# Two 16-head cross attentions: layer normalisation per batch, its shift by a product of two tensors, no opening product in the mixing, the last batch scaled by VectorE

## The reference, cut to what matters

```python
def cross_attention(x, context, w_q, b_q, w_k, b_k, w_v, b_v, w_o, b_o):   # context: (32, 77, 96)
    q = (x @ w_q + b_q).reshape(B, 128, 16, 8)          # 16 heads of 8
    k = (context @ w_k + b_k).reshape(B, 77, 16, 8)
    v = (context @ w_v + b_v).reshape(B, 77, 16, 8)
    scores = jnp.einsum('bqhd,bkhd->bhqk', q, k) / sqrt(8)
    weights = jax.nn.softmax(scores, axis=-1)
    out = jnp.einsum('bhqk,bkhd->bqhd', weights, v).reshape(B, 128, 128)
    return out @ w_o + b_o

x = layernorm(x + cross_attention(x, context, ...))     # (x - mean) / sqrt(var + 1e-5), no scale or bias
```

## Time and profile before

| | us |
|---|---|
| median of 3 runs | 3539.06 (3532.92 to 3542.62) |
| profiled execution, its own time | 3534.11 |
| its span, first to last instruction | 3532.3 |
| first cross attention, 1359.9 to 1560.6 | 200.7 |
| second cross attention, 3178.0 to 3378.7 | 200.7 |

### The profile page before, as it was taken

How to read it: one execution, slowest core, us unless ns; L and a number is a source line. 1 busy time by engine, 2 the same in 40 slices (tenths; PEclk the granted TensorE clock), 3 DMA queues, 4 the chain that set the end, 5 groups by cost and what they waited for, 6 DMA issues and landing times. The chain is left out here.

```text
span 3532.3 us, 80927 instructions
## 1 busy us (share of the span) xinstructions
PE 2729.6 (77%) x30395; PEld 1966.6 (56%) x30395; DVE 2442.8 (69%) x7116; ACT 1969.3 (56%) x3739; POOL 1545.0 (44%) x1205
## 2 busy tenths in 40 slices
PE   2899999987875957889899999956655656858846
PEld 1677777656564945556455555534433446845546
DVE  6688888866564968966666776649982553568945
ACT  2577777744443854765455655555432733556747
POOL 3555455412237823520165556623231257815544
PEclk9999999999976978989999999977766858978958
DMA  4333333311202211000000000000007012200013
GB/s 137 56 55 54 56 54 56 50 60 66 83 16 62 78 52 67 2 2 1 1 2 3 3 3 2 3 1 19 19 28 220 13 41 64 82 27 38 2 32 101
DMA packets 103278, 151.13 MB, mean 43 GB/s; under 512 B 26266, under 2 KB 76524, under 8 KB 101756
## 3 DMA queue, kind: packets, MB, share of 16 engines
q1 hardware_dynamic: 91546, 123.11, 14.1%
q0 software_dynamic: 10912, 22.70, 1.9%
q10 hardware_dynamic: 434, 0.15, 0.0%
HBM read 81.13 MB, written 49.04 MB: 37 GB/s over the span
## 5 line engine op out<-in xcount | busy, mean ns | idle before, releaser
L473 DVE TENSOR_REDUCE MX<-banks 128x8 f32<-128x1152 f32 x128 | 173.0, 1352 | 103.7 <-PE banks L290 103.6
L2469 POOL TENSOR_TENSOR SM<-SM,RZ 128x1232 f32<-128x1232 f32 x64 | 143.9, 2248 | 166.4 <-DVE RZ L2511 166.4
L1729 POOL DMA_INDIRECT sorted_rows<-SRC,IDX x160 | 156.7, 979 | 132.4 <-DVE IDX L1858 85.8
L442 POOL TENSOR_TENSOR KT<-KT,FL 128x512 f32<-128x512 f32 x64 | 81.6, 1275 | 304.0 <-DVE FL L462 304.0
L1742 POOL DMA_INDIRECT expert_results<-Y,DST x181 | 177.1, 979 | 81.8 <-DVE DST L1925 36.3
L399 ACT COPY PT<-banks 128x384 f32<-128x384 f32 x384 | 170.1, 477 | 48.6 <-PE banks L300 44.9
L1511 PE MATMUL banks<-XC,WR 128*128 128x128 f32 x1448 | 197.0, 280 | 0.2 <-ACT XC L1631 0.2
L300 PE MATMUL banks<-sb_c_ident,SM 128*128 128x128 f32 x1152 | 182.7, 286 | 9.8 <-ACT PT L399 9.4
L1511 PEld LDWEIGHTS banks<-XC,WR 128*128 128x128 f32 x1448 | 180.4, 196 | 2.5 <-ACT XC L1631 2.1
L2808 POOL TENSOR_TENSOR KQ<-T,EX 128x1024 f32<-128x1024 f32 x32 | 76.0, 2376 | 207.4 <-ACT EX L2789 207.4
L486 DVE TENSOR_TENSOR SM<-banks,MX 128x512 f32<-128x512 f32 x256 | 163.4, 679 | 0.0
(11 more groups left out here) (568 smaller groups left out, 8634.9 us busy)
## 6 DMA issues: line engine op xcount, KB each, us to landing
FL<-RAW SPq DMA_DIRECT2D x512, 64.0 KB, 2.3
sorted_rows<-in_zeros_dram SPq DMA_DIRECT2D x33, 528.0 KB, 8.5
XR<-sorted_rows SPq DMA_DIRECT2D x181, 66.0 KB, 1.9
SRC<-expert_results SPq DMA_DIRECT2D x16, 512.0 KB, 7.2
T<-s4d_k_dram SPq DMA_DIRECT2D x8, 1024.0 KB, 9.4
weight_region<-in_l_ffn__wall_dram SPq DMA_DIRECT2D x1, 4112.0 KB
film_dram<-F SPq DMA_DIRECT2D x8, 512.0 KB, 2.9
FO<-film_dram SPq DMA_DIRECT2D x8, 512.0 KB, 4.6
```

What stands on the lines that cost most here:

```text
L473: nc.vector.tensor_reduce(MX[:, n % 2], sc, AXX, ALU.max).then_inc(s.mx, 1)
L1729: nc.gpsimd.indirect_dma_start(out=rows, out_offset=bass.IndirectOffsetOnAxis(ap=IDX[:, k, t:t + 1], axis=0), in_=SRC[:, t, k, :], in_offs ...
L2469: nc.gpsimd.tensor_tensor(SM[:, t % 4], SM[:, t % 4], bc(RZ[:, t % 2, :].unsqueeze(2), [P, H, L]), ALU.mult).then_inc(s.nm, 1)
```

## The change

The normalisation of a group of four becomes four normalisations of one batch. At every step VectorE does one `bn_stats` and one `bn_aggr`, ScalarE one logarithm, one exponential and one application. The shift changes its form: ScalarE makes -mean by an `activation` with scale -1, and VectorE multiplies two [128, 1] tensors in SBUF with `tensor_tensor`. The zero product in front of the mixing goes, and the first product of each 32 rows opens its own sum instead. The multiplication of the last batch's weights by RZ moves from GpSimd to VectorE. The loops of VectorE and ScalarE run two steps longer.

```diff
+def dve_ln_stats_one(nc, dve, E, s, t, src):
+    st, mv = E.ln_stats[t // GB][:, t % GB, :], E.ln_mv[t // GB][:, t % GB, :]
+    nc.vector.bn_stats(st, src).then_inc(s.ln_stats, 1)
+    dve.wait_ge(s.ln_stats, t + 1)
+    nc.vector.bn_aggr(mv, st).then_inc(s.ln_var, 1)
+def act_ln_rstd_one(nc, act, E, s, t):
...
+    act.wait_ge(s.ln_var, t + 1)
+    nc.scalar.activation(std, mv[:, 1:2], ACT.Ln, bias=E.eps5[:]).then_inc(s.ln_std, 1)
+    nc.scalar.activation(st[:, 0:1], mv[:, 0:1], ACT.Identity, scale=-1.0)
+    act.wait_ge(s.ln_std, t + 1)
+    nc.scalar.activation(rstd, std, ACT.Exp, scale=-0.5).then_inc(s.ln_rstd, 1)
+def dve_ln_shift_one(nc, dve, E, s, t):
...
+    dve.wait_ge(s.ln_rstd, t + 1)
+    nc.vector.tensor_tensor(std, st[:, 0:1], rstd, ALU.mult).then_inc(s.ln_core, 1)
+def act_ln_apply_one(nc, act, E, s, t, src, dst):
...
+    act.wait_ge(s.ln_core, t + 1)
+    return nc.scalar.activation(dst, src, ACT.Identity, bias=std, scale=rstd)
...
-                        nc.tensor.matmul(z_bank, ZERO[:], ZERO[:], start=True, stop=False)
...
-    ins = nc.tensor.matmul(z_bank[32 * c:32 * (c + 1)], value_window(g, b, 4 * c + q), PT[:, t % 2, q, c, :], start=False, stop=q == 3)
+    ins = nc.tensor.matmul(z_bank[32 * c:32 * (c + 1)], value_window(g, b, 4 * c + q), PT[:, t % 2, q, c, :], start=q == 0, stop=q == 3)
...
-                    if i >= 8 and (i - 8) % GB == 0:
-                        act_rstd(nc, act, E, s, (i - 8) // GB)
-                    if i >= 9 and (i - 9) % GB == 0:
-                        g = (i - 9) // GB
-                        act_ln_apply(nc, act, E, s, g, grp(XB, g), grp(E.x, g))
+                    if 6 <= i < NB + 6:
+                        act_ln_rstd_one(nc, act, E, s, i - 6)
+                    if i >= 8:
+                        act_ln_apply_one(nc, act, E, s, i - 8, XB[:, i - 8, :], E.x[:, i - 8, :])
...
-                nc.gpsimd.memset(ZERO[:], 0.0).then_inc(s.one, 1)
...
-                    normalise(t)
+                    if t < NB - 1:
+                        normalise(t)
...
+                    if i == NB:
+                        t = i - 1
+                        dve.wait_ge(s.rz, t + 1)
+                        nc.vector.tensor_tensor(SM[:, t % 4], SM[:, t % 4], bc(RZ[:, t % 2, :].unsqueeze(2), [P, H, L]), ALU.mult).then_inc(s.nm_last, 1)
...
-                    if i >= 7 and (i - 7) % GB == 0:
-                        g = (i - 7) // GB
-                        dve.wait_ge(s.res, GB * (g + 1))
-                        dve_ln_stats(nc, dve, E, s, g, grp(XB, g))
-                    if i >= 9 and (i - 9) % GB == 0:
-                        dve_ln_shift(nc, dve, E, s, (i - 9) // GB)
+                    if 5 <= i < NB + 5:
+                        dve.wait_ge(s.res, i - 4)
+                        dve_ln_stats_one(nc, dve, E, s, i - 5, XB[:, i - 5, :])
+                    if 7 <= i < NB + 7:
+                        dve_ln_shift_one(nc, dve, E, s, i - 7)
```

More of the change, by code:

```diff
@@ L140, in act_ln_apply @@
     return ins
+def dve_ln_stats_one(nc, dve, E, s, t, src):
[4 more added lines that the diff above has]
+def act_ln_rstd_one(nc, act, E, s, t):
+    st, mv = E.ln_stats[t // GB][:, t % GB, :], E.ln_mv[t // GB][:, t % GB, :]
+    std, rstd = E.ln_std[t // GB][:, t % GB:t % GB + 1], E.ln_rstd[t // GB][:, t % GB:t % GB + 1]
+    act.wait_ge(s.ln_var, t + 1)
[4 more added lines that the diff above has]
+def dve_ln_shift_one(nc, dve, E, s, t):
+    st, std, rstd = E.ln_stats[t // GB][:, t % GB, :], E.ln_std[t // GB][:, t % GB:t % GB + 1], E.ln_rstd[t // GB][:, t % GB:t % GB + 1]
+    dve.wait_ge(s.ln_rstd, t + 1)
+    nc.vector.tensor_tensor(std, st[:, 0:1], rstd, ALU.mult).then_inc(s.ln_core, 1)
+def act_ln_apply_one(nc, act, E, s, t, src, dst):
+    std, rstd = E.ln_std[t // GB][:, t % GB:t % GB + 1], E.ln_rstd[t // GB][:, t % GB:t % GB + 1]
+    act.wait_ge(s.ln_core, t + 1)
+    return nc.scalar.activation(dst, src, ACT.Identity, bias=std, scale=rstd)
 def dve_ln_affine(nc, dve, E, s, k, src, dst, scale, shift):
@@ L2291, in xattn16 @@
     TAIL = 4 * L
-    with sublayer(nc, "xt_ps xt k_ps k kd v_ps v one q_ps q s_ps mx sub ex sm rz nm pt_ps pt z_ps zt o_ps rb res w_ld" + LN) as (s, ctx):
+    with sublayer(nc, "xt_ps xt k_ps k kd v_ps v one q_ps q s_ps mx sub ex sm rz nm nm_last pt_ps pt z_ps zt o_ps rb res w_ld" + LN) as (s, ctx):
         sb = E.scratch(ctx)
@@ L2296, in xattn16 @@
         MX = sb("MX", [P, 2, H]); SM = sb("SM", [P, 4, H, L]); PT = sb("PT", [P, 2, 4, 4, P])
-        ZERO = ctx.enter_context(nc.sbuf_tensor(f"zero_{nc.next_id()}", [1, P], BF16))
         SU = sb("SU", [P, 2, H]); RZ = sb("RZ", [P, 2, H]); ZT = sb("ZT", [P, 2, P])
@@ L2349, in weights_T @@
                     if a == 0:
-                        pe.wait_ge(s.nm, t + 1)
+                        if t < NB - 1:
+                            pe.wait_ge(s.nm, t + 1)
+                        else:
+                            pe.wait_ge(s.nm_last, 1)
                     if 2 * t + a >= 1:
@@ L2437, in weights @@
                     nc.scalar.copy(PT[:, t % 2, 2 * a:2 * a + 2].rearrange("k q c (r p) -> k (q c) r p", r=2), turned).then_inc(s.pt, 1)
-                for i in range(NB + 6):
+                for i in range(NB + 8):
                     t = i - 3
@@ L2455, in _ @@
                         nc.scalar.activation(SM[:, i % 4], SM[:, i % 4], ACT.Exp, scale=float(D) ** -0.5).then_inc(s.ex, 1)
-                    if i >= 8 and (i - 8) % GB == 0:
-                        act_rstd(nc, act, E, s, (i - 8) // GB)
-                    if i >= 9 and (i - 9) % GB == 0:
-                        g = (i - 9) // GB
-                        act_ln_apply(nc, act, E, s, g, grp(XB, g), grp(E.x, g))
+                    if 6 <= i < NB + 6:
+                        act_ln_rstd_one(nc, act, E, s, i - 6)
+                    if i >= 8:
+                        act_ln_apply_one(nc, act, E, s, i - 8, XB[:, i - 8, :], E.x[:, i - 8, :])
             @block.gpsimd
             def _(pool):
-                nc.gpsimd.memset(VZ[:], 0.0)
-                nc.gpsimd.memset(ZERO[:], 0.0).then_inc(s.one, 1)
+                nc.gpsimd.memset(VZ[:], 0.0).then_inc(s.one, 1)
                 def normalise(t):
```

## The result

| | before | after |
|---|---|---|
| median of the runs, us | 3535.99 (3525.19 to 3542.62, 4 runs) | 3590.73 (3588.16 to 3595.88, 4 runs) |
| ratio to before | | 1.016, 95% interval 1.013 to 1.0189 |
| profiled execution, span, us | 3532.3 | 3594.0 |
| first, second cross attention, us | 200.7, 200.7 | 230.5, 231.3 |

The changed kernel is 1.6% slower. The kernel before has a fourth run here (3525.19), which brings its median from 3539.06 down to 3535.99; the medians lie 54.7 us apart. The profiled executions lie 61.7 us apart, and that of the changed kernel is the slowest of its four. Of these 61.7 us of span, 29.9 and 30.6 lie in the two cross attentions (1364.19 to 1594.71 and 3207.89 to 3439.16), 1.3 in all the rest of the program.

The account below looks back on a forecast made before the run. VectorE was taken to set the pace, busy 19.98 of 21.0 us. Held shifts +66.9, statistics +1.5, zero vector -0.4 and end -3.8 gave +64.2 us, forecast 3600; own range 3588 to 3640, 8 in 10 3578 to 3655.

Parts of the forecast that it names:

- The held shift: VectorE's shift waits about 1.9 us for GpSimd's multiplication at 25 steps per cross attention, 6.80 us each; +66.9 us together.
- The bounds that I had left: Limits for a one-column shift's duration beside GpSimd: 0.15 us if not held, 1.9 if held throughout; upper end taken.
- The dividing line: Claim that VectorE instructions with two SBUF inputs are held beside GpSimd; a tensor_tensor with one PSUM input is not.
- The small terms: Parts beside the hold: statistics +1.5 us, zero vector's clearing -0.4, end -3.8; zero product and last batch 0.
- the zero product: Dropping it from TensorE's mixing gains nothing in the pipeline; at most -13 us if TensorE set the pace.
- the last batch: Its multiplication on VectorE, 1.44 us for GpSimd's 2.25, is hidden: 0, at most -0.8 us each time.
- Statistics, end and zero vector: Statistics at steps 5 and 6 +1.5 us; shorter end of both sublayers -3.8; clearing the zero product's operand gone -0.4.
- the 25 gaps: Intervals between reciprocals of batches 6 and 31 in each cross attention; forecast 170.6 us, before 138.3 and 136.0.
- The sum: All terms together, 66.9 + 1.5 - 0.4 - 3.8 = +64.2 us on the profiled execution's 3534.1.
- The rival with TensorE as bound: TensorE sets the pace if its clock falls below 0.68; at 0.60, +45 us, 3645; chance 0.10.
- The hold over the group's work: Hold also lasts through GpSimd's bias and keys, 3.5 us at 6 steps per sublayer, +42 us; chance within 0.02.
- The rival in which the shift passes: The one-column shift is not held beside GpSimd, taking 0.15 us: -10 us, median some 3529; chance 0.13.

Follow-up runs that it names:

- e1: Changed kernel with the shift as a one-column tensor_scalar, rstd as scalar operand, at the same place; 3516.3 us, ratio 0.9959.
- e2: Changed kernel with the same tensor_tensor shift directly behind the reciprocal, ahead of the residual addition and statistics; 3519.5 us, ratio 0.9965.
- e3: Changed kernel with the shift made by ScalarE and no VectorE instruction for it; 3512.3 us, ratio 0.9946.
- e4: Changed kernel with the one-column shift as scalar_tensor_tensor, still two SBUF tensors, at the same place; 3592.8 us, ratio 1.0171.
- e7: e3 with the zero product and its vector's clearing on GpSimd put back; 3512.27 us, ratio 0.9953.
- e5: Kernel before, without the zero product and with the last batch's weights multiplied on VectorE, normalisation unchanged; 3526.1 us, ratio 0.9996.
- e8: Changed kernel with GpSimd's multiplication of a batch's weights split into two instructions of 8 heads; 3548.4 us, ratio 1.0056.
- e10: e6 with the group's shift moved right behind the subtraction of the same step, 1.77 us sooner; 3511.4 us, ratio 0.9955.
- e11: e6 with a group's four applications on ScalarE spread over four steps, one each; 3513.4 us, ratio 0.9957.
- e6: Kernel before with the group's shift as four one-column tensor_scalar instead of one scalar_tensor_tensor of four columns; 3536.4 us, ratio 1.0005.

## Why the prediction was right

The forecast was 3600, the median is 3590.7, near the lower end of the range of 3588 to 3640 and on the side forecast.

**The held shift**: right in place, length and count. 1.87 us against 1.9; a step of 6.80 against 6.80; 170.1 against 170.6; +65.9 against +66.9. e1, e2, e3 and e4 show that the hold alone makes the loss: e4, which keeps it, has 3592.8; without it or with a fifth of its holds, all else left per batch, the same chip gives 3512.3 to 3519.5, some 73 to 81 us less. The bounds that I had left, 0.15 us to 1.9, were both real, for a `tensor_scalar` and a `tensor_tensor`; to go by the row of the same place was right. The dividing line was too simple: two inputs in SBUF are held, but so is a `tensor_scalar` of four columns with one (L2845). The forecast does not hang on that, because the shift of the changed kernel has two.

**The small terms**: the zero product at nothing is right where VectorE sets the pace (e7); for the last batch, and for both in the kernel before, e5 leaves up to some 6 us open. Statistics, end and zero vector together I put at -2.7; the two sublayers outside the 25 gaps came out at 60.4 - 65.9 = -5.5. Up to the reciprocal of batch 6 it is +0.7; the other -6.2 lie behind that of batch 31, where I had -3.8. The last addition to the end is 3.23 us for 3.4 forecast, so the rest lies in how the last batches run through. Which edit gave it I did not separate.

**The sum**: +61.7 in the spans for +64.2. Most of the 9 us by which 3600 is too high is the base: I went up from the profiled execution of before by 2 us to a median, and that of the changed kernel lies 5 below its profiled 3595.88.

**The rival with TensorE as bound** falls: the clock did drop, to 0.86 and 0.88, above the 0.68 from which it was to decide; TensorE waits for VectorE, up to 2.72 us at a time, and VectorE for nobody. **The hold over the group's work** falls too: the hold ends with one instruction (e8, e2).

**The rival in which the shift passes** was mispriced, though it did not happen. I put it at -10; e1, which is that case, gave -14.2 (3530.5 to 3516.3), and e3 -18.2. For its 25 gaps I had 130.9 + 25 x 0.1 = 133.4 us, from an undisturbed group of 21.30; in e1 they take 127.9. That group was not as undisturbed as I read it (VectorE was busy 19.98 of 21.0 us, and e10's groups take 20.76): VectorE waited for TensorE in it, 0.24 us once and 0.47 here:

```profile
3284.32 1.44 DVE L2518 TENSOR_REDUCE MX<-banks 128x16 f32<-128x1232 f32 x1 [0.47 <-PE banks L2344]
```

So VectorE sets the pace of the kernel before only in the main; e11, which against e6 changes ScalarE's list alone, shows that the lists of the others count there too. And the groups of before were not slow by the holds alone, as I had it. In the group with the held shift of the earlier trace rows, ScalarE and then TensorE waited longer still than in e6:

```profile
1486.85 1.65 ACT L139 ACTIVATE x_res<-x_res,ln_std,ln_rstd 128x128 f32<-128x128 f32 x4 [1.57 <-DVE ln_std L131]
1488.41 0.99 ACT L2437 COPY PT<-banks 128x1024 f32<-128x1024 f32 x1
```

```profile
1489.45 0.72 PE L2358 MATMUL banks<-sb_c_ident,SM 64*128 64x64 f32 x16 [1.80 <-ACT PT L2437]
```

e6 took away the hold, kept that chain in every group and gained nothing; e10 and e11 broke the chain, and so does any shift per batch that is not held (e1, e3).

## What to carry to other kernels

Ahead of a VectorE instruction, count the tensors that it reads from SBUF and ask what GpSimd does at that moment: with two, even a single column pays for all that is left of GpSimd's running instruction. What helped here: a `tensor_scalar` of one column, another engine, or a place just ahead of GpSimd's start. Wider `tensor_scalar`s were held too, so look at the trace before relying on a scalar operand. When a stall that sits in one engine's list is taken away and nothing is gained, follow who waited on its result: here four applications behind a late shift starved TensorE of its copy. Sooner or spread did it, each by itself.

## What the runs showed of the hardware

- The hold goes by instruction, not by GpSimd's queue: with two halves back to back the shift took 834 ns in the median instead of 1867, and was done when the first half ended (1.22 us).
- Its size does not depend on the held instruction's: one column (1867 ns) as four columns before (1.87 to 1.93 us).
- One tensor from SBUF is no safeguard: a `tensor_scalar` of four columns took 1.0 us or more in seven of seven cases beside GpSimd, 0.17 without it; of one column (e1) it took 0.18 in the midst of GpSimd's 2.25 us.
- A lead of 0.16 us is enough: at 3243.77 the product passes ahead of GpSimd's start at 3243.93 in 0.10 us.
- TensorE, busy 1.54 of 3.00 us behind one wait of 1.36 us, was granted 0.50 of its clock over the next 6.70 us, and the engine that had set the pace then waited for it.
